# Centring the dense rows with one bfloat16 product each, the mean carried in three bfloat16 parts, in a graph layer on one Trainium2 core

## The reference

```python
deg = maximum(segment_sum(ones, dst, N), 1); s = deg ** -0.5
h = maximum((x - mean(x)) / sqrt(var(x) + 1e-5), 0)        # per row of 128
msg = (h[src] @ W1 + (h[src] * h[dst]) @ W2) * (s[src] * s[dst])
a = segment_sum(msg, dst, N) + h @ W1
a = where(a >= 0, a, 0.2 * a)
out = x + a / maximum(norm(a), 1e-12)                       # norm per row
```

## Time and profile before

| | us |
|---|---|
| median of 3 runs | 928.2 (927.44 to 931.21) |
| profiled execution, its own time | 928.79 |
| its span, first to last instruction | 927.1 |
| busy: DVE | 870.1 (94%) |
| busy: PE / PEld | 734.7 (79%) / 713.7 (77%) |
| busy: ACT | 711.0 (77%) |
| busy: POOL | 682.0 (74%) |
| mean granted clock of TensorE | 0.912 of full speed |

### The profile page before, as it was taken

The page is one execution under the profiler, slowest core; times in us unless marked ns, Lnnn a source line. Parts: engine busy times, 40 slices in busy tenths (PEclk is TensorE's granted clock), DMA queues, the critical chain, the costliest instruction groups (busy, mean ns, idle before and its releaser), DMA issues.

```text
span 927.1 us, 21508 instructions
## 1 busy us (share of the span) xinstructions
PE 734.7 (79%) x6104; PEld 713.7 (77%) x6104; DVE 870.1 (94%) x2878; ACT 711.0 (77%) x2944; POOL 682.0 (74%) x694
## 2 busy tenths in 40 slices
PE   1499888888987988888878898798798887988820
PEld 1398878888887987888877888798788887988810
DVE  6789999999999999999999999999999999999980
ACT  0079887797887987887879788797888888779950
POOL 1777888888788788787788887888888887833472
PEclk9999998898998998998989899898999999889965
DMA  2813746646645655755754664675665665653532
GB/s 71 304 50 90 242 155 196 232 162 201 237 163 197 238 173 188 241 181 180 234 201 164 209 236 165 207 239 165 207 238 168 200 247 166 210 201 131 172 138 60
DMA packets 68804, 172.90 MB, mean 186 GB/s; under 512 B 14383, under 2 KB 34514, under 8 KB 62434
## 3 DMA queue, kind: packets, MB, share of 16 engines
q1 hardware_dynamic: 49868, 135.41, 43.1%
q0 software_dynamic: 18816, 36.08, 12.7%
HBM read 96.89 MB, written 77.04 MB: 188 GB/s over the span
## 4 chain that ended last, share of the span: by engine, by line
DVE 79%; issue 10%; PE 3%; ACT 3%; DMA 1%; DVEq 1%; POOL 0%; SPq 0%; POOLq 0%; ACTq 0%
DVE bst L784 20%; DVE xo L829 19%; DVE ybuf L837 10%; DVE cjk L753 7%; DVE agg L859 5%; DVE oe L821 5%; DVE ye L942 3%; DVE ge L745 2%; DVE ge L746 2%; ACT junk L973 1%; DMA xin<-in_x 1%; PE pt L1106 1%; DVE scs L876 1%; DVE rd L907 1%; DVE d L765 1%
## 5 line engine op out<-in xcount | busy, mean ns | idle before, releaser
L1106 PE MATMUL pt<-nident,bst 128*128 128x128 f32 x1568 | 300.5, 296 | 0.0
L467 POOL DMA_INDIRECT out<-oe,sstage x196 | 234.7, 1198 | 60.3 <-issue 59.1
L1106 PEld LDWEIGHTS pt<-nident,bst 128*128 128x128 f32 x1568 | 265.0, 212 | 0.0
L462 POOL DMA_INDIRECT xs<-in_x,stage x196 | 215.5, 1099 | 53.3 <-issue 52.7
L462 POOL DMA_INDIRECT xd<-in_x,stage x196 | 208.8, 1065 | 59.7 <-issue 59.7
L1116 PE MATMUL pu<-w,ct 128*128 128x128 f32 x1568 | 222.5, 293 | 22.4 <-ACT ct L957 22.4
L1103 PE MATMUL pt<-ident,xin 128*128 128x128 f32 x784 | 230.8, 294 | 7.9 <-DVE bst L784 4.8
L973 ACT ACTIVATE junk<-ybuf 128x128 bf16<-128x128 f32 x784 | 233.3, 306 | 0.7 <-DVE ybuf L837 0.7
L829 DVE SCALAR_TENSOR_TENSOR xo<-ybuf,rd,xin 128x128 f32<-128x128 f32 x784 | 226.6, 341 | 0.0
L1116 PEld LDWEIGHTS pu<-w,ct 128*128 128x128 f32 x1568 | 202.3, 205 | 29.4 <-ACT ct L957 25.8
L957 ACT ACTIVATE ct<-pt 128x512 f32<-128x512 f32 x196 | 116.3, 593 | 55.1 <-PE pt L1106 53.9
(11 more groups left out here) (136 smaller groups left out, 1165.2 us busy)
## 6 DMA issues: line engine op xcount, KB each, us to landing
xin<-in_x SPq DMA_DIRECT2D x96, 512.0 KB, 4.5
out<-xo SPq DMA_DIRECT2D x48, 1024.0 KB
srow<-src_rows SPq DMA_DIRECT2D x49, 256.0 KB, 6.9
edge_rows<-oe SPq DMA_DIRECT2D x49, 256.0 KB
same<-same_segment SPq DMA_DIRECT2D x49, 128.0 KB, 6.2
xs<-in_x,stage POOLq DMA_INDIRECT x196, 2.9
xd<-in_x,stage POOLq DMA_INDIRECT x196, 3.7
out<-oe,sstage POOLq DMA_INDIRECT x196
```

The lines of the kernel that those rows point to most:

```text
L462: pool.indirect_dma_start(out=to, out_offset=None, in_=rows, in_offset=bass.IndirectOffsetOnAxis(ap=index, axis=0), bounds_check=limit, oo ...
L467: pool.indirect_dma_start(out=out, out_offset=bass.IndirectOffsetOnAxis(ap=index, axis=0), in_=rows, in_offset=None, bounds_check=row_limi ...
L1106: last = pe.matmul(pt[:, q % 2, f], mean[:, s.buf(0, 2), col:col + 1].to_broadcast([P, D]), nident[:], start=False, stop=True)
```

## The change

The mean of each dense row is a float32 word. Its upper 16 bits, read as bfloat16, are its leading part. `mean_rest` (two DVE subtractions per step over 128x16 words) puts mean minus leading part into word 0 of `bst`, and that minus its own leading part into word 2; the upper halves of the three words are then three bfloat16 numbers whose sum is the mean. Once per step TensorE turns these 48 columns with one bfloat16 product against `identb` into `pe_m` (`turn_means`), and ACT copies the 48x128 result to `mt` as bfloat16 (`copy_means`). The centring product of each block then has `pickb`'s column as weights (48 rows, -1 in the three rows of that block's mean, spread over 128 columns) and `mt` as the moving side: one bfloat16 product with 48 rows in place of a float32 one with 128 rows, which stands as two instructions in the profile. DVE's next statistics wait for `mt_done`, one TensorE product, in place of `t_done`. In the setup `pick` is made by a reduction of `ident`, and ACT makes the two bfloat16 constants.

```diff
-        nident = sb("nident", [P, P])
+        identb = sb("identb", [P, P], BF16)
+        pick = sb("pick", [3 * TD, TD])
+        pickb = sb("pickb", [3 * TD, TD], BF16)
+        mt = sb("mt", [3 * TD, P], BF16)
...
+        parts = [bst[:, h, 0:TD * 3].bitcast(BF16)[:, 1::2] for h in range(2)]
+        upper = bst[:, :, 0:TD * 3].rearrange("p b (t w) -> p b w t", w=3)
...
-            dve.tensor_scalar(nident[:], ident[:], -1.0, None, ALU.mult).then_inc(s_const, 1)
+            thirds = ident[0:3 * TD, 0:3 * TD].rearrange("p (t w) -> p t w", w=3)
+            dve.tensor_reduce(pick[:], thirds, AX.X, ALU.add, negate=True).then_inc(s_const, 1)
...
+            def mean_rest(s, d, k):
+
+                b = s.buf(d, 2)
+                dve.wait_ge(bn_done, s(d + 1))
+                if k:
+                    dve.wait_ge(rest_done, s(d + 1))
+                word, to = ((mean[:, b, 0:TD], upper[:, b, 0, :]), (upper[:, b, 0, :], upper[:, b, 2, :]))[k]
+                high = bst[:, b, 0:TD * 3].bitcast(BF16)[:, (3 if k == 0 else 1)::6]
+                dve.tensor_tensor(to, word, high, ALU.subtract).then_inc((rest_done, parts_done)[k], 1)
...
             stats_guard(Step(0, 0), 0)
+            for k in range(2):
+                mean_rest(Step(0, 0), 0, k)
...
                     if has(i, -1):
-                        dve.wait_ge(t_done, s() * NQ)
+                        dve.wait_ge(mt_done, s())
                     stats_dense(s, 1, 0, 4, i)
...
                 if has(i, 1):
                     stats_guard(s, 1)
+                    mean_rest(s, 1, 0)
...
                     if has(i, 1):
                         stats_edges(s, 1, k)
+                        if k == 0:
+                            mean_rest(s, 1, 1)
...
         def _(act):
+            act.wait_ge(s_const, 1)
+            act.copy(identb[:], ident[:])
+            act.copy(pickb[:], pick[:]).then_inc(s_pick, 1)
+            def copy_means(s, d):
+
+                act.wait_ge(mt_done, s(d + 1))
+                act.copy(mt[:], pe_m[0:3 * TD, 0:P]).then_inc(mt_evac, 1)
+
             act.wait_ge(dg_done, 1)
             act.activation(dd[:], d2[:], ACT.Sqrt).then_inc(dd_ready, 1)
+            copy_means(Step(0, 0), 0)
...
                 if has(i, 0):
                     copy_quarter(3)
+                if has(i, 1):
+                    copy_means(s, 1)
...
+            def turn_means(s, d):
+
+                pe.wait_ge(parts_done, s(d + 1))
+                pe.matmul(pe_m[0:3 * TD, 0:P], parts[s.buf(d, 2)], identb[:], start=True, stop=True).then_inc(mt_done, 1)
+
+            pe.wait_ge(s_pick, 1)
+            turn_means(Step(0, 0), 0)
...
-                        last = pe.matmul(pt[:, q % 2, f], mean[:, s.buf(0, 2), col:col + 1].to_broadcast([P, D]),
-                                         nident[:], start=False, stop=True)
+                        if q == 0 and t == 0:
+                            pe.wait_ge(mt_evac, s(1))
+                        last = pe.matmul(pt[:, q % 2, f], pickb[:, col:col + 1].to_broadcast([3 * TD, P]), mt[:], start=False, stop=True)
...
                 if has(i, 0):
-                    pe.wait_ge(bn_done, s(1))
+                    pe.wait_ge(x_loaded[s.buf()], s.dma() + more(i, 0))
+                    pe.wait_ge(x_loaded2[s.buf()], s.dma() + more(i, 0))
                     turn_quarter(0)
...
                     mul_quarter(3)
+                if has(i, 1):
+                    if has(i, -1):
+                        pe.wait_ge(msg_done, s())
+                    turn_means(s, 1)
+                if has(i, 0):
                     h = s.buf(0, 2)
                     pe.wait_ge(relu_done, s(1))
```

More of the change, by code:

```diff
@@ L204, in gnn_preln_kernel @@
         s_const = sem("s_const")
+        s_pick = sem("s_pick")
         s_ch = sem("s_ch")
@@ L267, in gnn_preln_kernel @@
         ye_done = sem("ye_done")
+        rest_done = sem("rest_done")
+        parts_done = sem("parts_done")
+        mt_done = sem("mt_done")
+        mt_evac = sem("mt_evac")
         t_done = sem("t_done")
```

## The result

The changed kernel takes 963.9 us (median of 4 runs, 953.3 to 977.7), the kernel before 929.0 in the same comparison: **2.8% slower**, a ratio of 1.028 with an interval of 1.025 to 1.030. That ratio takes the two shorter runs, 953.3 and 957.4 us at a granted clock of 0.866 and 0.863; the other two took 970.4 and 977.7 at 0.844 and 0.826. The prediction was 931.6 us, range 929.0 to 938.0, so it was wrong: even the shortest run is 21.7 us above it, five times the largest term of its sum (4.3 us). The profiled execution took 953.3 us.

The account below looks back on a forecast made before the run. DVE was taken to bound the kernel, with PE waiting for it. Second subtraction +4.3, steps 0 and 1 +0.2, start -1.1, the rest 0: +3.4 on 928.79 gives 932.2, as a median 931.6 us; range 929.0 to 938.0.

Parts of the forecast that it names:

- The bound now: Whole kernel: DVE's queue paces it from about 89 to 872 us, 17.32 us a step, while PE waits for DVE.
- What leaves PE: PE's centring blocks: a cheaper product saves 0.11 to 0.17 us a block, some 1.8 to 2.7 us a step.
- I price this at zero on the path: PE's saving per step: worth 0, since its 2.01 us wait for DVE's masks only grows to 4 to 4.5.
- The clock: Rival: PE stays at 1.2 GHz after longer waits, +3.6 us a step, over 1080 us in all; chance 0.03.
- Second subtraction: DVE, between edge statistics and edge output: uncovered, 0.09 us a step, +4.3 us in all, bounds +1.0 to +9.1.
- First: First subtraction on DVE, between `guard` and edge output: hidden behind `rd`, 0; +4.3 us if the cover fails.
- the large rival (0.33): Both subtractions lie open on DVE between `guard` and edge output: +9.8, so 938.0 us, or from 933; chance 0.33.
- In the loop: The 24 steps run with registers: the subtractions cost nothing extra there, 0, with 24 x 0.08 = +1.9 us as other end.
- New waits at 0: PE's turn of the means, ACT's copy, the next centring product and `mt_done`: all covered, 0 us.
- Start: Steps 0 to 2: first turn some 2 us later but shorter, fewer DVE waits; -1.1 us, bounds -2.5 and +1.
- The sum: All terms on the profiled 928.79 us: +3.4, so 932.2, and 931.6 as a median, +0.4%.

Follow-up runs that it names:

- e2: The changed kernel with the means' table filled with zeros to 128 rows, same values: 930.95 us, 1.0017 of the kernel before; 0.979 to 0.990 where that took 1267 to 1302.
- e6: The changed kernel with its table zero-filled to 128 rows and five centring products a block of alternating sign: 937.3 us, 1.009; 1.070 on a slow chip.
- e4: The kernel before with DVE's two subtractions added and their results unused: 934.3 us, 1.0048; 1.018 and 1.005 in the comparisons with the slow kernel before.

## Why the prediction was wrong, and where it was right

- **The bound now: right.** PE waited for DVE, and e2 with PE relieved keeps that.
- **What leaves PE: this step failed.** I took the new product to cost 0.05 to 0.11 us after the nearest rows, four lookups of 128 rows in a row. None of these products has another number of rows than its neighbours, and the changed kernel goes from 128 to 48 and back in every block. A block at full clock costs 0.42, not 0.16 to 0.22; "PE saves 1.8 to 2.7 us a step" was in truth 16 x 0.09 = 1.4 us more. "I price this at zero on the path" rested on a wait growing from 2.01 to 4 us; it shrank from 94.8 to 28.2 us in sum instead. With 128 rows (e2) the block is 0.17, inside the forecast; but PE's busy time, which was to fall by 100 us or more, falls by 76 even there (658.9 for 734.7).
- **The clock: the rival was named, with the wrong condition.** I leaned on unbroken work raising the clock and keeping it up. With blocks full of products it was up (e6, 0.97); in the changed kernel PE has no gap from 785 to 877 us and still drops to 1.2 GHz. That rival's price, over 1080, was for good; the low clock came in stretches, at a cost of 15 to 18 us by e6. Its 0.03 was too little, and none of my cases had PE itself getting more work.
- **Second subtraction: right.** 0.08 a step for 0.09; e4 +4.5 us in all. **First: right**, hidden in the shadow of `rd`, so the large rival (0.33) didn't come about. **In the loop: right** for all I can see.
- **New waits at 0: right with 128 rows.** In e2 DVE waits for PE for 3.8 + 2.0 us, before for 5.1 + 2.0.
- **Start: right in e2** (DVE's third scan at 87.17 for 89.11 us: -1.9, for -1.1 in bounds of -2.5 to +1), wrong in the changed kernel: +5.6 us at the same place (94.72 for 89.11). The first turn starts 2.2 us later, as I took (44.33 for 42.15), but the first eight blocks take 0.62 us each, not the 0.32 that I took and that e2 shows, so they win nothing on the 0.64 of before. PE's rows then reach full clock only at about 52 us, where those of before do at 47, and the blocks behind that take 0.42 for 0.33.
- **The sum** was that of e2: 931.6 forecast, 930.95 measured. As a difference to the kernel before it was +3.4 forecast and +1.6 measured; 0.8 of the 1.8 between them are the start (-1.9 for -1.1). So the closeness of the two times is in part luck: the kernel before took 929.3 beside e2, and 928.2 when I forecast. For the changed kernel one term was mis-sized, PE's, which stood in the sum at zero.

## What to carry to other kernels

A product with 48 rows is not cheaper beside ones with 128 rows; fill its operands up with zeros (1.0017), or put such products in a row (1.0044). For other numbers of rows, measure. A busy share of PE near 100% can be weight loads and products in turn: compare the start of each load with that of its product. And before a step is priced at "none, that engine waits anyway", put the worst case of the operation against the wait, not only the nearest row: 16 blocks with 0.09 us more and a lower clock ate the 2 us of cover.

## What was not expected of the hardware

- Each change between products of 128 and of 48 rows costs 0.09 to 0.13 us at 2.4 GHz; 128 rows throughout, none.
- PE's clock fell to 1.2 GHz behind eight blocks in which loads and products take turns, without a gap in the records; the mean clock from 94 to 785 us was 0.88 so, and 0.97 with blocks of nearly the same length full of products.
- VectorE stopped at the loop's jump for 1.3 to 6.1 us in all; with 8 and with 24 instructions put ahead in its program it was 6.1 and 1.4.
- In three comparisons the kernel before took 1267 to 1302 us, for a reason not found; PE stopped amid its streams in the traces from there, and in one of them the change cost 1.11 times.
